# State scan of a Mamba layer: products of the odd states with their C row made in token layout by TensorE turns and ScalarE scaled copies

## The reference, cut to what matters

```python
dt = softplus(einsum("brl,dr->bdl", dt_low, dt_proj_w) + dt_proj_b)
A = -exp(A_log)                                    # 256 channels x 16 states
for each token t:
    dA = exp(dt_t[..., None] * A)
    state = state * dA + (dt_t * u_t)[..., None] * B_t[:, None, :]
    y_t = einsum("bdn,bn->bd", state, C_t)         # sum over the 16 states
y = (y + D * u) * silu(z)
x = x + tanh(g_xattn[0]) * y
```

## Time and profile before

| | |
|---|---|
| median of 3 runs | 576.02 us (575.34 to 576.35) |
| profiled execution | 575.79 us, span 573.8 us |
| busy: TensorE, VectorE, ScalarE, GpSimd | 481.4, 472.5, 364.4, 279.7 us |
| scans (L1884) | 64, 77.9 us together |
| products with C (L1893) | 64, 42.3 us together |
| additions (L1277) | 128 instructions, 72.8 us |
| decays (L831), B copies (L839) | 64, 44.1 us; 32, 18.6 us |
| B times du on GpSimd (L586) | 64, 81.3 us |

### The profile page before, as it was taken

How to read it: one execution, slowest core, us unless ns; L and a number is a source line. 1 busy time by engine, 2 the same in 40 slices (tenths; PEclk the granted TensorE clock), 3 DMA queues, 4 the chain that set the end, 5 groups by cost and what they waited for, 6 DMA issues and landing times.

```text
span 573.8 us, 10348 instructions
## 1 busy us (share of the span) xinstructions
PE 481.4 (84%) x3106; PEld 363.5 (63%) x3106; DVE 472.5 (82%) x1249; ACT 364.4 (64%) x831; POOL 279.7 (49%) x263
## 2 busy tenths in 40 slices
PE   6817777757889899999899999998699988998835
PEld 3302222222368766776888999987589888997714
DVE  4899999999997838788567857896899969875887
ACT  2785555435526555787676666679556796689544
POOL 4118777869520555630287368623874243333111
PEclk9956999999999999999899999999999999999876
DMA  5939400001045889893422012400335000000000
GB/s 155 228 84 324 125 0 1 1 1 37 1 136 154 272 256 295 233 306 104 167 58 63 1 38 57 56 2 1 53 57 61 0 2 2 19 2 1 0 20 19
DMA packets 45626, 48.63 MB, mean 85 GB/s; under 512 B 5660, under 2 KB 42118, under 8 KB 45574
## 3 DMA queue, kind: packets, MB, share of 16 engines
q1 hardware_dynamic: 41734, 36.46, 22.7%
q0 software_dynamic: 3840, 11.54, 9.1%
HBM read 41.43 MB, written 6.56 MB: 84 GB/s over the span
## 4 chain that ended last, share of the span: by engine, by line
PE 32%; DVE 23%; issue 22%; POOL 10%; ACT 7%; DMA 3%; SPq 1%; DVEq 1%; POOLq 0%; ACTq 0%
DVE hst L1884 7%; PE ps L1628 5%; PE ps L1567 3%; PE ps L1568 3%; PE ps L1569 3%; PE ps L1617 2%; POOL G L672 2%; POOL dbu L586 2%; POOL pn L688 2%; PE ps L1277 2%; PE ps L1485 2%; DVE hc L1893 2%; DMA G<-token_rows,idx_x 1%; POOL G L650 1%; PE ps L1521 1%
## 5 line engine op out<-in xcount | busy, mean ns | idle before, releaser
L688 POOL TENSOR_TENSOR pn<-pr,pinv 128x512 f32<-128x512 f32 x64 | 67.6, 1058 | 88.3 <-DVE pinv L2293 87.8
L586 POOL TENSOR_TENSOR dbu<-du,brow 128x512 f32<-128x512 f32 x64 | 81.3, 1282 | 41.6 <-DVE du L1877 23.1
L1277 PE MATMUL ps<-hc,ident 128*128 128x512 f32 x128 | 72.8, 657 | 27.2 <-DVE hc L1893 25.7
L1884 DVE TENSOR_TENSOR_SCAN hst<-ps,dbu 128x512 f32<-128x512 f32 x64 | 77.9, 1217 | 0.2 <-POOL dbu L586 0.2
L831 ACT ACTIVATE ps<-dtv,amat 128x510 f32<-128x510 f32 x64 | 44.1, 690 | 49.1 <-DVE hst L1884 48.2
L1019 ACT ACTIVATE pr<-ebuf,smin 128x256 f32<-128x256 f32 x128 | 63.7, 502 | 13.5 <-POOL pn L688 6.7
L1628 PE MATMUL ps<-pT,cS 128*128 128x256 f32 x256 | 66.5, 382 | 0.0
L1277 PEld LDWEIGHTS ps<-hc,ident 128*128 128x128 f32 x128 | 20.3, 195 | 66.9 <-DVE hc L1893 63.7
L650 POOL DMA_INDIRECT G<-token_rows,idx_x x32 | 37.7, 1179 | 44.2 <-DVE wkv L2019 20.8
L672 POOL DMA_INDIRECT G<-expert_out,idx_g x48 | 51.2, 1066 | 11.6 <-issue 10.7
L2284 DVE CUSTOM_DVE_ANT_0 ebuf<-ps,mbias 128x256 f32<-128x256 f32 x128 | 49.0, 420 | 5.9 <-issue 5.8
(11 more groups left out here) (380 smaller groups left out, 1384.3 us busy)
## 6 DMA issues: line engine op xcount, KB each, us to landing
wdn<-in_L_ffn_wd SPq DMA_DIRECT2D x12, 384.0 KB
wgu<-in_L_ffn_wg SPq DMA_DIRECT2D x11, 384.0 KB
wgu<-in_L_ffn_wu SPq DMA_DIRECT2D x11, 384.0 KB
expert_out<-xn SPq DMA_DIRECT2D x11, 256.0 KB
wq<-in_L_xattn_Wq SPq DMA_DIRECT2D x2, 1024.0 KB, 9.3
wo<-in_L_xattn_Wo SPq DMA_DIRECT2D x1, 2048.0 KB, 15.8
wo<-in_L_ffn_w SPq DMA_DIRECT2D x2, 1024.0 KB, 7.0
expert_out<-pexp SPq DMA_DIRECT2D x5, 256.0 KB
```

Of the source, the lines that this page charges most:

```text
L586: nc.gpsimd.tensor_tensor(dbu[:, j, :], du[:, j % 2, 512 * hb:512 * hb + 512], brow[:, j // 2, :], ALU.mult).then_inc(pool_dbu, 1)
L688: nc.gpsimd.tensor_tensor(pn[:, h % 2], pr[:, h % 2], pinv[:, h % 2, :].unsqueeze(2).to_broadcast([P, 2, L]), ALU.mult)\
L1277: pe.matmul(bank(2 + j % 2), ident[:], hc[:, j % 2, :], start=(isinstance(m, int) and m + k == 0), stop=(isinstance(m, int) and m + k == N ...
L1884: V.tensor_tensor_scan(hst[:, j, :], bank(j % 2), dbu[:, j, :], 0.0, ALU.mult, ALU.add)\
```

## The change

For the odd state of every pair but the very last, the product with C is no longer made in channel layout by VectorE. After a pair's four scans, TensorE turns the odd state's two pieces into token layout, 128 x 128 at a time, through bank 7 in two halves of 256 tokens (`turn_states`); in token layout C's value is one number per partition, so ScalarE makes the product as a copy with a scale (`scale_turned`, two copies of 128 x 256 per half, into `z_first` and `z_second`); and TensorE turns the scaled halves back by products with the identity that add right into the sums in banks 2 and 3 (`turn_back`). The C values in token layout (`c_rows`) come from 16 small products made ahead of the scan in bank 7. The C row of an odd state is spread no longer, except for the last one, whose two pieces go the old way. VectorE's queue has the two remaining products of a pair at other places. The layer work of the first half is placed anew between the rounds. Two semaphores (`f_mean`, `f_last`) are used for the new waits, and their later counts are raised by what these add. SP waits for `c_rows` to be in PSUM before it loads Wq.

```diff
-            def decays(hb, m):
-                for j in range(4):
-                    decay(hb, m, j)
-                    if j % 2:
-                        copy_b(hb, m + 1, j // 2)
+            def scale_turned(hb, m, half):
+
+                pair = NS // 2 * hb + m
+                act.wait_ge(z_in_psum, 2 * pair + half + 1)
+                if half == 0:
+                    wait_count(act, y_added, 4 * pair if isinstance(pair, int) else 4 * pair + 1)
+                act.wait_ge(z_copied, 1)
+                for q in range(2):
+                    last = A((z_first, z_second)[half][:, q, :], bank(7)[:, DT * P * q:DT * P * q + DT * P], ACT.Copy,
+                             scale=c_rows[:, 4 * hb + 2 * half + q, bass.ds(2 * m + 1, 1)])
+                last.then_inc(z_copied, 1)
+
+            def decays(hb, m, between):
...
+                decay(hb, m, 0)
+                decay(hb, m, 1)
+                if first:
+                    take_c_rows()
+                else:
+                    scale_turned(*before, 0)
+                if not last:
+                    copy_b(*after, 0)
+                between(0)
+                decay(hb, m, 2)
+                if not first:
+                    scale_turned(*before, 1)
+                decay(hb, m, 3)
+                if not last:
+                    copy_b(*after, 1)
+                between(1)
...
+            for c in range(NT):
+                for d in range(DT):
+                    last = pe.matmul(bank(7)[:, NS * c:NS * c + NS], u[:, d, P * c:P * c + P], xpT[:, d, NS:2 * NS],
+                                     start=(d == 0), stop=(d == 1))
+            last.then_inc(winT_in_psum, 1)
...
+            def turn_states(hb, m, half):
+
+                pair = NS // 2 * hb + m
+                if half == 0:
+                    pe.wait_ge(scanned, 4 * pair + 4)
+                pe.wait_ge(z_copied, 2 * pair + half + 1)
+                for q in range(2):
+                    for d in range(DT):
+                        at = DT * P * half + P * q
+                        last = pe.transpose(bank(7)[:, DT * P * q + P * d:DT * P * q + P * d + P],
+                                            hst[:, 2 + d, at:at + P], ident[:])
+                last.then_inc(z_in_psum, 1)
+
+            def turn_back(hb, m, stop=False):
+
+                pair = NS // 2 * hb + m
+                pe.wait_ge(z_copied, 2 * pair + 3)
+                for d in range(DT):
+                    for c in range(4):
+                        done = pe.matmul(bank(2 + d)[:, P * c:P * c + P],
+                                         (z_first, z_second)[c // 2][:, c % 2, P * d:P * d + P], ident[:],
+                                         start=False, stop=stop and c == 3)
+                    done.then_inc(y_added, 1)
...
+            def state_pair(hb, m, to_c, to_b, between):
...
+                if late:
+                    turn_states(hb, m, 0)
+                add_out(hb, m, 0, start=first)
+                if not late:
+                    turn_states(hb, m, 0)
+                add_out(hb, m, 1, start=first)
+                spread_c(*to_c, 0)
+                between(0)
+                turn_states(hb, m, 1)
+                if to_b:
+                    spread_b(*to_b, 0)
+                    spread_b(*to_b, 1)
+                turn_back(hb, m, stop=last)
+                between(1)
...
                 dve.wait_ge(da_ready, i + 1)
                 dve.wait_ge(pool_dbu, i + 1)
-                wait_count(dve, hc_ready, i - 3)
+                before = NS // 2 * hb + m - 1
+                if isinstance(before, int) and before < 0:
+                    pass
+                elif j < 2:
+                    dve.wait_ge(hc_ready, 2 * before + j + 1)
+                else:
+                    dve.wait_ge(z_in_psum, 2 * before + 2)
...
-            def scan_four(hb, m, first):
-                for j in range(4):
-                    scan(hb, m, j)
-                    if j:
-                        read_out(hb, m, j - 1)
-                    elif not first:
-                        read_out(hb, m - 1, 3)
+            def scan_four(hb, m, between):
+
+                scan(hb, m, 0)
+                scan(hb, m, 1)
+                read_out(hb, m, 0)
+                between(0)
+                scan(hb, m, 2)
+                scan(hb, m, 3)
+                between(1)
+                read_out(hb, m, 1)
```

More of the change, by code:

```diff
@@ L107, in build_program @@
         ebuf = sb("ebuf", [P, 8 * H])
+        with ExitStack() as turned_scope:
+            z_first = sb("z_first", [P, 2, DT * P], F32, turned_scope)
         hT = sb("hT", [I, 2, 2 * P])
@@ L862, in take_folded, with no_more, routing @@
                     .then_inc(mn_copied, 1)
+            def no_more(k):
+                return
             copy_b(0, 0, 0)
             copy_b(0, 0, 1)
[L866 to L880, removed]
+            decays(0, 0, no_more)
+            with act.Fori(1, NS // 2) as m:
+                decays(0, m, no_more)
+            for m in range(NS // 2):
+                def routing(k):
+                    if 2 * m + k == 12:
+                        rows_turned(0, 0)
+                    if 2 * m + k == 14:
+                        rows_turned(0, 1)
+                    if 2 * m + k == 15:
+                        exps_of(0)
+                decays(1, m, routing)
             for n, k in enumerate((2, 3, 0, 1)):
@@ L1397, in _ @@
[L1397 to L1402, removed]
-                    spread_b((n + 4) // NS, (n + 4) % NS // 2, k)
-                if n == NS + 3:
-                    turn_out(0, 0)
-                if n == NS + 4:
-                    turn_out(0, 1)
-                if n == NS + 8:
-                    turn_normal(0, 0)
-                if n == NS + 10:
-                    turn_normal(0, 1)
-                if n == NS + 12:
-                    logits_of(0)
+            def state_pair(hb, m, to_c, to_b, between):
+                whole = isinstance(m, int)
+                late = whole and hb and m == 0
+                first, last = whole and m == 0, whole and m == NS // 2 - 1
+                if late:
[12 more added lines that the diff above has]
+                between(1)
@@ new lines, in no_more, with routing @@
+            def no_more(k):
+                return
+            state_pair(0, 0, (0, 1), (0, 2), no_more)
+            with pe.Fori(1, NS // 2 - 2) as m:
+                state_pair(0, m, (0, m + 1), (0, m + 2), no_more)
+            for m in range(NS // 2 - 2, 2 * (NS // 2) - 1):
+                def routing(k):
+                    n = 2 * m + k - NS
+                    if n == 3:
+                        turn_out(0, 0)
+                    if n == 5:
+                        turn_out(0, 1)
+                    if n == 9:
+                        turn_normal(0, 0)
+                    if n == 12:
+                        turn_normal(0, 1)
+                    if n == 13:
+                        logits_of(0)
+                state_pair(*divmod(m, NS // 2), divmod(m + 1, NS // 2),
+                           divmod(m + 2, NS // 2) if m + 2 < NS else None, routing)
@@ L1414, in _ @@
+            spread_c(1, NS // 2 - 1, 1)
+            for j in range(4):
+                add_out(1, NS // 2 - 1, j, stop=(j > 1))
             pe.wait_ge(d_kv, 32)
```

108 lines of the change are left out of this document (57 added, 51 removed).

## The result

| | before | after |
|---|---|---|
| median | 575.71 us (575.34 to 576.35, 4 runs) | 594.99 us (592.91 to 595.35, 4 runs) |
| profiled execution | 575.79 us, span 573.8 us | 595.09 us, span 593.1 us |
| busy: TensorE, VectorE, ScalarE, GpSimd | 481.4, 472.5, 364.4, 279.7 us | 501.1, 459.1, 386.2, 279.1 us |
| first scan; summing up of the second half | 44.1; 162.1 us | 44.9; 180.7 us |

The ratio is 1.0323, interval 1.0306 to 1.034: slower by 19 us. The forecast of 586.5 us had the sign and lies inside 575 to 598, but it saw 10.7 of 19.3 us.

A forecast was written before the change was run, and what follows sets the result against it. VectorE was taken to set the scan's pace before, a closed chain of TensorE and ScalarE waits after. Terms 3.8 + 1.2 + 2 + 1 + 2.7 = 10.7 us on 575.79 gave 586.5 us, range 575 to 598.

The forecast's parts named there:

- ring: Scan stage: TensorE and ScalarE wait on each other in a closed chain, 7.1 us per pair of states, +3.8 us.
- the loop's waits: Scan's hardware loops: ScalarE starts later after its release, in some six rounds, 6 x 0.2 = +1.2 us.
- clock at the stage's start: Start of the scan stage: TensorE, still at 1.2 GHz, takes double time for its links, +2 us (0 to +5).
- second half, ring and layer work together: Second half of the scan: 7 x 0.25 us from the ring, plus layer work's +1 (-2 to +3); +2.8 us.
- the end: From last pair's first scan to the summing up: logits stand ahead of the last additions, 12.5 us, +2.7 (0 to +3.5).
- behind the summing up: After the scan stage: order of work unchanged, so the stage's gain or loss reaches the end whole; 0 of its own.
- the signs: Mid-stage: VectorE about 80% busy, rounds 7.1 to 7.4 us, ScalarE's spread wait 0.9 to 1.0 us, TensorE's wait over 1 us.
- the third rival: TensorE stays at 1.2 GHz in the loop: each of six rounds grows by 4.1 us, 611 us; chance 0.10.
- The rule on turns: TensorE's turns in transpose mode do not count as busy work for its clock; from the Trainium skill, no size given.
- C rows and SP's wait: Ahead of the scan: small products for C rows and SP's wait before Wq cost nothing; without cover up to 4 us.

The follow-up runs named there:

- the fill: Changed kernel plus four unused bf16 products in TensorE's wait ahead of the turn back, first half of the tokens; 588.37 us, ratio 1.0225.
- written out: Changed kernel with the hardware loops of the scan's first half unrolled on all four engines; 586.34 us, ratio 1.0204.
- The fill with turns: Changed kernel plus eight unused 128x128 turns in TensorE's wait ahead of the turn back, first half of the tokens; 591.47 us, ratio 1.0244.

## Why the forecast had the sign and half of the size

Part by part, from the first scan of each kernel; the sums are of the profiled executions.

| | forecast | measured |
|---|---|---|
| ahead of the first scan | 0 | +0.8 |
| ring in the first half's eight rounds, without the loop's waits | +2.0 | +2.0 |
| the loop's waits | +1.2 | +2.0 |
| clock at the stage's start | +2 | +0.8 |
| falls of the clock in the loop | 0 | +5.0 |
| second half, ring and layer work together | +2.8 | +5.3 |
| the end | +2.7 | +2.7 |
| behind the summing up | 0 | +0.7 |
| total | +10.7 | +19.3 |

(The ring's +3.8 is split into 8 x 0.25 for the first half and 7 x 0.25 for the second, where the layer work's +1 joins it. First half: 64.4 us with falls, 58.6 with the fill, 56.6 written out, 54.6 before; second half 58.9 against 53.6. The rows of the first half are these differences, the clock's 5.8 split as under the fill. Behind the summing up the traces of kernels whose edit doesn't touch that part take 410.0 to 413.6 us, so +0.7 is no effect.)

**The ring: right.** It was put at 7.1 us; the links without the loop measure 7.17 (1.89, 0.86, 0.64, 3.78), and the 0.1 above the forecast is the turn back's (1.89 for 1.79). Four kernels that shorten it by its own logic shorten the round, to 6.65 (twice), 6.68 and 5.66 us, where 6.7, 6.65, 6.7 and 5.7 had been worked out. The +2.0 of the first half agrees by some luck: it is six rounds of 0.32 and nothing in the two at the start, and not eight of 0.25. That all engines had slack by sums said nothing. Of the signs, VectorE is busy 73%, where about 80 was named; ScalarE's wait for the spread is 0.96 to 1.05 us, at the top of 0.9 to 1.0; the loop's undisturbed rounds are 7.50, just over 7.1 to 7.4; TensorE's wait ahead of the turn back is 0.86 to 0.94, and over 1 was named.

**The loop's waits: mechanism right, size off.** 0.33 us a round over six rounds, where 0.2 was taken: the scaled copy alone starts 0.23 later, and spread, copy and second copies 0.10.

**The clock: the step that failed.** The forecast weighed two states: slow at the stage's start (+2, measured 0.8), or slow through the whole loop (the third rival, 611 us). What came is between them: rounds at full clock and rounds with a fall take turns, three of the latter in the loop and one in the second half. The sum had nothing for them. The argument against the rival, that after a fall the dense stretch brings the clock back, was right, and so was the observation behind the rival, that the new round has gaps; I had made them exclude each other. Nor was it the price I gave it: a fall costs 1.66 us and not 4.1, since it lasts only for part of a turn back (+0.94) and one addition (+0.72). Three such falls came in the kernel with the logits moved too, in rounds 3, 5 and 7 of the first half (9.13, 9.14, 9.16 us) and not in 3, 6 and 8.

**The rule on turns.** The trace of before agreed with it as far as it went: twenty turns that did not raise the clock. The fill with turns does not: 8 turns a round in place of 4 products kept the granted clock at 1.00 in the loop. That is a test of keeping the clock up among other work, not of raising it; in it turns did not count less. What came is described elsewhere on the same page (the Trainium skill, TensorE: Matmul & The Clock Gate, Part 1, A second HAM failure mode): a TensorE that idles briefly between groups of products can swing between its two clock levels and lose in the swings. The trace agrees: 0.79, 1.00 and 0.79 stand in neighbouring stretches (80 to 104 us), with the same two waits in every round. What makes one wait end in a fall and the next not, with rows that read alike, the runs don't show.

**The second half: at the top of its bounds.** Layer work was put at 6.7 us beyond the ring (3.7 to 8.7 by the term's bounds); it measures 58.9 - 7 x 7.17 = 8.7. In it are a fall of the clock (0.82 in 152 to 160 us, 1.00 before) and the round of 9.3 us with GpSimd's rows; before, GpSimd was as full there (8.00 of 8 in 128 to 136) and VectorE too. In the changed kernel GpSimd spends 31.5 us waiting for ScalarE's B copies, so I read the difference as a lost lead; that was not tested by itself, and the attempt to take the rows from GpSimd met other costs.

**The end: right to 0.1 us**, 12.48 for 12.5, and moving the logits took 1.9 off. Its parts were off both ways, though: 6.5 us to the logits for 7, 1.9 for them, and 4.0 from the last additions to the summing up for 3.6. That a gain there reaches the time whole was wrong, as the two kernels with moved logits show; a loss did (+18.6 at the summing up, +19.3 in all).

**C rows and SP's wait: nothing, as said**, as far as they can be told apart. The 0.8 us ahead of the first scan are there at 25 us already, when TensorE starts on `dtlow` (24.92, before 24.12), ahead of the small products. Their cause stays open.

## What to carry to other kernels

When work moves from a full engine to two idle ones, list for each new operation what stands ahead of it in its queue and walk the loop that these waits make; sums of busy time can't show it. Then look for the link that waits for more than it needs: a wait split in two, at the same work, took 20 us off here, and a copy and a spread moved behind the ring's next link took as much. Part of each 20 us was the clock's falls. TensorE pays for its gaps twice, since its clock may fall behind them: here the loop's falls were 5.0 us, and unused work in the gap removed them. With six of eight products left out the gap stayed at 0.86 us, and one fall remained in the loop.

## What the runs showed of the hardware

- With two waits of TensorE in every round of 7.5 us, 0.87 and 0.86 us, the granted clock falls in some rounds and not in others that look the same; 0.9 us of unused work in the second wait, products or turns alike, removed every fall from the loop.
- Instructions that wait for another engine start 0.1 to 0.2 us later in a hardware loop than written out; in a ring of several such waits that is 0.33 us a round of 7.5.
- Four rows of 128x256 that VectorE normalises take 395 to 481 ns each at 158 us, with no product of GpSimd's beside them. At 124 us two start beside GpSimd's products and take 1239 and 1349 ns; they end 0.15 us after the product that was running beside each (125.42 after 125.27, 126.69 after 126.54), and the two behind the last product take 401 and 399 ns. So the length is a wait for GpSimd's product. The Trainium skill, GPSIMD Engine Reference, Specifications, says that GpSimd shares its SBUF interfaces with VectorE, with contention for some of VectorE's instructions (in 2-port modes, or with two SBUF inputs); the trace agrees that such rows contend, and doesn't show their mode.
